# Taking the moments of the second norm's first half behind the second half's key-value masking on VectorE

## The reference, cut to what matters

```
q, k = phi(h @ wq + bq), phi(h @ wk + bk)      # phi(t) = elu(t) + 1
v    = h @ wv + bv
kv   = einsum('bshd,bshm->bhdm', k, v)         # one 8x8 matrix a head and sequence
z    = 1 / (einsum('bshd,bhd->bsh', q, k.sum(axis=1)) + 1e-6)
att  = einsum('bshd,bhdm,bsh->bshm', q, kv, z)
h    = ln(h + att @ wo + bo, g1, be1)          # the first norm
y    = gelu(h @ w1 + c1) @ w2 + c2
h    = ln(h + y, g2, be2)                      # the second norm
```

## Time and profile before

| what | value |
|---|---|
| median of 3 runs | 1065.08 us (1064.76 to 1065.31) |
| the profiled execution, its own time | 1067.03 us |
| its span | 1065.3 us |
| granted TensorE clock, mean over the span | 0.976 of full speed |
| busy: TensorE (PE) / weight loads (PEld) | 997.0 us (94%) / 932.4 us (88%) |
| busy: VectorE (DVE) / ScalarE (ACT) / GpSimd (POOL) | 830.9 us (78%) / 831.4 us (78%) / 770.0 us (72%) |
| chain that ended last, by engine | PE 72%, POOL 6%, DVE 6%, issue 5%, DMA 4%, SPq 4%, ACT 2% |

### The profile page before, as it was taken

How to read it: one execution, slowest core, us unless ns; L and a number is a source line. 1 busy time by engine, 2 the same in 40 slices (tenths; PEclk the granted TensorE clock), 3 DMA queues, 4 the chain that set the end, 5 groups by cost and what they waited for, 6 DMA issues and landing times.

```text
span 1065.3 us, 25018 instructions
## 1 busy us (share of the span) xinstructions
PE 997.0 (94%) x7558; PEld 932.4 (88%) x7558; DVE 830.9 (78%) x2733; ACT 831.4 (78%) x1621; POOL 770.0 (72%) x1157
## 2 busy tenths in 40 slices
PE   5899999999999999999999999999998859989993
PEld 4799989999999999989999999899997759889993
DVE  6777887888888878887888788787889888953545
ACT  5878887888888888888888888888887645765582
POOL 5866877787877778777777777777766677677753
PEclk9999999999999999999999999999999878999997
DMA  4101263136314432443144315501302345667363
GB/s 140 51 1 36 55 130 60 36 75 111 59 38 96 90 59 42 99 90 60 40 100 100 63 42 122 95 8 21 100 1 80 93 130 162 178 190 219 102 182 129
DMA packets 196371, 92.81 MB, mean 87 GB/s; under 512 B 119788, under 2 KB 179187, under 8 KB 196112
## 3 DMA queue, kind: packets, MB, share of 16 engines
q1 hardware_dynamic: 190352, 81.71, 32.9%
q0 software_dynamic: 4544, 8.47, 2.3%
q10 hardware_dynamic: 1344, 1.05, 0.3%
HBM read 42.98 MB, written 31.54 MB: 70 GB/s over the span
## 4 chain that ended last, share of the span: by engine, by line
PE 72%; POOL 6%; DVE 6%; issue 5%; DMA 4%; SPq 4%; ACT 2%; DVEq 0%; POOLq 0%; ACTq 0%
PE psum L1943 19%; PE psum L1820 8%; PE psum L1822 8%; PE psum L1821 8%; PE psum L1867 6%; PE psum L1901 5%; PE psum L1873 5%; PE psum L1855 4%; PE psum L2102 4%; POOL xs L929 4%; PE psum L2086 4%; SPq L508 3%; DMA this_w<-w 2%; DVE stat L1240 1%; PE psum L1964 1%
## 5 line engine op out<-in xcount | busy, mean ns | idle before, releaser
L1026 ACT ACTIVATE s<-s,shift,rstd 128x128 f32<-128x128 f32 x496 | 203.9, 485 | 40.7 <-POOL shift L761 40.3
L1943 PE MATMUL psum<-this_w,hid 128*128 128x128 f32 x1792 | 216.5, 277 | 3.0 <-DMA this_w<-w 3.0
L1943 PEld LDWEIGHTS psum<-this_w,hid 128*128 128x128 f32 x1792 | 208.5, 193 | 4.2 <-DMA this_w<-w 4.2
L1005 ACT ACTIVATE hid<-psum,col 128x512 f32<-128x512 f32 x256 | 155.2, 683 | 2.3 <-PE psum L1822 1.7
L759 POOL TENSOR_TENSOR rstd<-var,neg_half 128x4 f32<-128x4 f32 x132 | 146.3, 1108 | 11.0
L802 POOL TENSOR_TENSOR res_a<-s,row 128x512 f32<-128x512 f32 x60 | 77.4, 1290 | 73.6 <-ACT s L1026 68.4
L1240 DVE BATCH_NORM_STATS2 stat<-s 128x6 f32<-128x128 f32 x512 | 110.0, 277 | 0.0
L756 POOL TENSOR_SCALAR shift<-mv 128x4 f32<-128x4 f32 x132 | 25.8, 195 | 100.1 <-DVE mv L1244 98.8
L1820 PE MATMUL psum<-x_hi,this_w 128*128 128x512 f32 x224 | 95.5, 426 | 1.2 <-DVE x_lo L1312 1.2
L787 POOL TENSOR_TENSOR res_f<-res_f,row 128x512 f32<-128x512 f32 x64 | 92.3, 1443 | 5.0
L2102 PE MATMUL psum<-heads,hid 128*128 x624 | 86.7, 284 | 6.8 <-ACT hid L1158 5.6
(11 more groups left out here) (270 smaller groups left out, 2761.3 us busy)
## 6 DMA issues: line engine op xcount, KB each, us to landing
xs<-pad SPq DMA_DIRECT2D x18, 975.0 KB, 8.8
feature<-xrow SPq DMA_DIRECT2D x416, 32.0 KB, 2.0
res_a<-w SPq DMA_DIRECT2D x28, 256.0 KB
xblk<-xs SPq DMA_DIRECT2D x78, 65.0 KB
row<-rows SPq DMA_DIRECT2D x8, 512.0 KB, 5.4
raw_w<-w SPq DMA_DIRECT2D x15, 256.0 KB, 3.0
this_w<-next_w SPq DMA_DIRECT2D x7, 512.0 KB, 3.2
this_qkv<-next_qkv SPq DMA_DIRECT2D x6, 384.0 KB, 2.9
```

Of the source, the lines that this page charges most:

```text
L1005: a.activation(hid[h][:, c, :], ps(3 + h + c), ACT.Gelu, bias=col[:, bass.ds(lw * FF + (C_C1 + c), 1)]).then_inc(hid_done, 1)
L1026: ins = a.activation(dst[:, t, :], src[:, t, :], ACT.Identity, bias=shift[i][:, t:t + 1], scale=rstd[i][:, t:t + 1])
L1943: ins = t_.matmul(ps(down_bank(l, s, h))[:, t * P:(t + 1) * P], hid[h][:, c, t * P:(t + 1) * P], down[:, c, :], start=c == 0, stop=c == FF ...
```

## The change

On VectorE `moments2(l, s - 2, 0)`, four `bn_stats` and four `bn_aggr` a slot, is called behind `mask_kv(l, s, 1)` and no longer in front of `lo_x1(l, s - 1, 1)`. So `lo_x1(1)` and `mask_kv(1)` stand ahead of it now, in slot 31 also `sum_moments(0)`, and `attend(0)` directly behind it. The instructions and their waits are the same, and no other engine's program is touched.

```
--- before.py
+++ after.py
@@ -1495,8 +1495,6 @@
                 keys(l, s, 1)
                 if first and s == 0:
                     start(7)
-                if p2:
-                    moments2(l, s - 2, 0)
                 if p1:
                     lo_x1(l, s - 1, 1)
                 if first and s == 0:
@@ -1505,6 +1503,8 @@
                 if last and s == 3:
                     sum_moments(0)
                 mask_kv(l, s, 1)
+                if p2:
+                    moments2(l, s - 2, 0)
                 attend(l, s, 0)
                 attend(l, s, 1)
                 if last and s == 3:
```

## The result

The changed kernel takes **1082.44 us** (median of 4 runs, 1080.14 to 1084.7) against 1064.92 for the kernel before in the same comparison: ratio **1.0161, interval 1.0137 to 1.0186**, 17.5 us slower. The forecast, 1082 us, held. The profiled execution took 1083.48 us with a span of 1081.8, 16.5 more than the profiled one before; the sum of the prediction was 16.8.

A forecast was written before the change was run, and what follows sets the result against it. TensorE, busy nearly throughout the layers, was taken to bound the kernel. Plain slots 13.3, second 3.0, third -1.6 and slot 31 2.1 gave 16.8 us more than the median 1065.1: 1082 us, range 1070 to 1090.

The forecast's parts named there:

- What bounds the kernel: Through the layers TensorE is busy nearly all the time, 94.9 of 96 us; only its waits can be gained or lost.
- The gap at L1867: TensorE's weight load for `attention(0)` waits for VectorE's `lo_x1(1)`; the whole 0.27 us a slot should go.
- `mask_kv(1)` stays, GpSimd starts 1.4 us later, nothing absorbs it: `mask_kv(1)` follows TensorE's products; moments come 2.4 us later, GpSimd and the lane to `lo_moved` 1.4 us later.
- 0.95 us in fourteen plain slots: First and fourth slots with `lo_moved`, plus 28 and 29: `add_res1(1)` and TensorE's `flip_x1(0)` 0.95 us late, 13.3 us together.
- 0.5 us in second slots: Six second slots of a layer: transfer waits and VectorE slack leave 0 to 0.95, taken as 0.5; 3.0 us together.
- Slots 26, 27 and 30: nothing: GpSimd later still, the gap absent, or the forward flip waiting for `norm2(0)` as much as was gained: 0.
- 2.1 us in slot 31: Last slot: late moments delay `norm2(0)`, `scale_resid(0)` and `sum_inv(0)` on the chain that ends last, +2.1 us.
- third ones: Six third slots of a layer: VectorE's slack covers the 1.4 us delay, the gain stays, 6 x -0.27 = -1.6 us.
- the covered lane: Rival: GpSimd and ScalarE catch the moments up, only the gap at `attention(0)` goes, 7.5 us: 1057.6 us; chance 0.08.
- What L809 adds to `lo_moved`: GpSimd's `offset_resid(0)` lengthens `lo_moved` from an undisturbed 1.37 us; extra 0.67 for 0.89 overlap, forecast 0.5, so 1.87 us.
- the prediction's doubt of the rule: At `lo_moved`, full port blocking would make the extra the whole overlap, 0.2 us more a slot; rows showed 0.67 of 0.89.
- The third rival: Much slower: TensorE waits some 1.4 us in plain slots and its granted clock falls too, 23 us more, 1105 us; chance 0.06.

The follow-up runs named there:

- the early version: Against the kernel before, the moments moved the other way, in front of `mask_kv(0)`: 1058.65 us, ratio 0.9953.
- the kernel with the moments later still: Against the changed kernel, the moments moved one step further back, behind `attend(0)`: 1137.22 us, ratio 1.0689 to the kernel before.

## Why the prediction was right

- **What bounds the kernel**: right. In the layers the loss is what TensorE waits: 21.0 us more at L1873, 7.5 less at L1867.
- **The gap at L1867 is a wait for `lo_x1(1)`, worth 0.27 us**: right. The row is gone, third slots (6, 10, 14, 18, 22) became 0.25 to 0.38 us shorter, and the early version keeps the gain in 24.50 us slots.
- **`mask_kv(1)` stays, GpSimd starts 1.4 us later, nothing absorbs it**: right. `lo_moved` starts 9.20 us behind `mask_kv(1)`; the prediction had 441.96 - 432.74 = 9.22.
- **0.95 us in fourteen plain slots**: right in sign and cause, too large. `lo_moved` took 1.70 us and not 1.87, and the first slots had 0.37 us to spare, not 0.28. Start +1.38, length -0.34, less 0.37 is 0.67 in slot 16 (measured 0.66); +1.59, -0.55, less 0.29 is 0.75 in slot 15 (measured 0.75). The fourteen sum to 10.2 us and not 13.3. `lo_moved` was shorter than forecast because the overlap with L809 was: L809 starts 8.47 us behind `mask_kv(1)` and not 7.43, 1.04 later (forecast 1.2 to 1.4), while `lo_moved` starts 1.38 later, and 0.54 us of overlap remain (forecast 0.7).
- **0.5 us in second slots**: too small. Slots 9, 13, 21 and 25 lost 0.66, 0.87, 0.96 and 1.13, slot 17 only 0.23. The slack was read from slot 17, where TensorE's weight loads waited 0.9 us for a transfer, more than in any of the other four (0.5 at most); and behind `lo_moved` the prediction followed VectorE alone, while in these slots GpSimd's end of the lane, with `sum_rows` in it, arrives last. The waits for transfers differ from run to run: against the 24.77 to 24.99 us of these five slots in the runs that move the moments in other slots alone, the changed kernel's 25.95 to 25.98 are 1.0 to 1.2 us more in each of them, slot 17 too, over the forecast's upper end of 0.95. Slot 5 became 1.6 us shorter: its granted clock stayed at 1.00, while in the profiled run before it had fallen there.
- **Slots 26, 27 and 30: nothing**: right for two (-0.03 and -0.08), wrong for slot 30, which lost 0.83. Its `flip_x2(0)` waits for `norm2(0)` directly:

```profile
805.30 0.42 PEld L1873 LDWEIGHTS psum<-ident,s 128*128 128x128 f32 x4 [1.11 <-ACT s L1026]
```

- **2.1 us in slot 31**: right, 6.72 - 4.70 = 2.02.
- Together, of the 16.5 us: 10.2 in plain slots (13.3 predicted), 2.2 in second ones with slot 5's -1.6 among them (3.0), -1.7 in third ones (-1.6), 0.7 for 26, 27 and 30 (0), 2.0 in the last (2.1). That is 13.4; the other 3 us are 1.6 in slot 0, which two of the experiments' runs have too and the others have not, and 1.4 in the routed part. So the total came this near partly because misses cancel, and partly by what single profiled runs happened to have in slots 0, 5 and 17: that part is luck.
- **The rivals**: the covered lane would have wanted `lo_moved` no more than 0.29 to 0.37 us later; its end came 1.04 later. The clock didn't fall in the plain slots; TensorE's waits at L1873 stayed at 1.6 us and under.
- **What L809 adds to `lo_moved`**: wrong in how it was read, though the 1.87 us it gave were only 0.17 off. The 1.37 us of slot 18 were not free of L809: it ran into them for 0.23 us, as it did for 1.12 in slot 15 (kernel before, slots 15 and 18, to be held against the earlier trace rows):

```profile
415.38 1.27 POOL L809 TENSOR_TENSOR res_a<-res_a,row 128x512 f32<-128x512 f32 x1
...
490.81 1.28 POOL L809 TENSOR_TENSOR res_a<-res_a,row 128x512 f32<-128x512 f32 x1
```

  With `offset_resid(0)` out of the way `lo_moved` takes 1.29 us. Against that the extra is 0.98, 0.75 and 0.08 us in slots 15, 16 and 18 of the kernel before and 0.41 in slot 16 of the changed one, for overlaps of 1.12, 0.89, 0.23 and 0.54: not a share of the overlap, but the overlap less 0.13 to 0.15. In all four `lo_moved` ends 1.14 to 1.16 us behind the end of L809.
- By **the Trainium skill** (SBUF — State Buffer, Who interferes with whom), a VectorE instruction with two SBUF inputs and a GpSimd one that reads SBUF contend for ports that are locked exclusively. The four rows agree, but for the 0.13 to 0.15 us; the prediction's doubt of the rule came from the 1.37. Not every GpSimd instruction did this: the power of `inv_std2(1)` (L759, 128x4) ran for 0.40 of the 1.29 us above, and `lo_moved` took the same 1.29 in slots 5 and 9 of the run with `inv_std2(0)` ahead of the weight work, where that power was over.

## What to carry to other kernels

Moving work behind a later step helps the step that comes forward and delays whoever consumes the moved work; look up how long the consumer already waits. If it waits, the delay is paid, less the slack where its lane comes back to the bounding engine. Work whose input has long been ready goes into an earlier wait of its engine instead: the same gap closed, 5 us faster where this change was 17.5 slower. And follow a lane to every engine on which it ends, in more than one slot: one slot with an odd transfer gave the wrong slack here. Where a duration is taken as undisturbed, look at what the other engine did in it: the 1.37 us of `lo_moved` were not.

## What was not expected

That the clock is so near to falling. In the run with `offset_resid(0)` out of the way it fell to 0.57 over 380 to 384 us behind a wait of 2.5 us, and again in slot 17 behind another of 2.5 (0.77 and 0.80 over 484 to 492 us); behind waits of 1.9 to 2.1 us in slots 9, 21 and 25 of the same run it kept 1.00, and so it did from 100 to 700 us of the kernel with the moments later still, whose waits in front of `flip_x1(0)` reached 2.1. But the length of a wait doesn't decide alone: in slot 5 the clock fell in the profiled run before, behind a wait of 2.4 us for weights, and in the changed kernel it stayed, behind one of 2.7 (waits from 152 to 182 us, then the stretch, of the changed kernel):

```profile
PEld psum L1943 <- DMA this_w<-w: 2.7, 1, 2.7
```

```profile
150.00:180.00 30.00, 27.52 (x200) 25.29 (x199) 22.46 (x62) 24.48 (x48) 23.20 (x34) 1.00 0.41 82
```

The third rival of the prediction exists. The changed kernel's waits in front of `flip_x1(0)`, 1.6 us at most, are shorter than any in the layers behind which a run here lost the clock (2.4 us and more); that this is what kept its clock at 1.00 is not shown.
